# A four-layer graph network on one core: the first phase sums messages by a scan, ScalarE forms all product parts, gathers read kept index tables

## The reference: what is computed

```python
h = jnp.maximum(_layernorm(x, axis=-1), 0.0)
# layer 0: src, dst get a self loop for every node
deg = segment_sum(ones, dst);  dinv = rsqrt(deg)
xw = h @ W
agg = segment_sum(xw[src] * (dinv[src] * dinv[dst])[:, None], dst) + b
x = x + where(agg >= 0, agg, prelu_a * agg)
# layer 1: x = x + segment_sum(edge_weight * h[src], dst) @ W.T + b
# layer 2: attention over the incoming edges, batch norm over all nodes, relu
# layer 3: an edge network and a node network on the edges' end points, segment_sum, relu
```

## Time and profile before

| What | us |
|---|---|
| median of 3 runs | 2609.81 (2604.56 to 2611.62) |
| profiled execution, its own time | 2608.14 |
| span in it, first to last instruction | 2606.6 |

### The profile page before, as it was taken

One profiled execution on the slowest core, in us unless ns is written; L12 is line 12 of the kernel. 1 busy time (PEld: TensorE's weight loads), 2 busy tenths in 40 slices (PEclk: granted clock), 3 DMA queues, 4 the chain that ended last, 5 costly groups with the idle time before them and its releaser, 6 DMA issues. The chain is left out here.

```text
span 2606.6 us, 48448 instructions
## 1 busy us (share of the span) xinstructions
PE 1899.9 (73%) x9715; PEld 1275.5 (49%) x9715; DVE 2027.9 (78%) x8016; ACT 1725.7 (66%) x4230; POOL 1311.4 (50%) x1309
## 2 busy tenths in 40 slices
PE   2445668888855666578884899566663999999996
PEld 1134445555534555468883444233332555555553
DVE  6855579999968999688885888588885777777773
ACT  3655679999965777589991444699994444444441
POOL 6755656666637666277760000000002677777773
PEclk9878889999986888889996999799997999999998
DMA  7989986666645777556662443699996544445540
GB/s 134 220 147 183 153 203 193 198 195 195 194 130 159 222 223 224 176 165 198 201 181 72 128 129 86 185 305 308 305 308 215 128 100 107 106 113 114 115 106 21
DMA packets 376244, 446.18 MB, mean 171 GB/s; under 512 B 103667, under 2 KB 225338, under 8 KB 376082
## 3 DMA queue, kind: packets, MB, share of 16 engines
q1 hardware_dynamic: 309970, 368.09, 50.8%
q0 software_dynamic: 59840, 74.08, 12.3%
q10 hardware_dynamic: 6272, 2.06, 0.5%
HBM read 288.86 MB, written 185.03 MB: 182 GB/s over the span
## 5 line engine op out<-in xcount | busy, mean ns | idle before, releaser
L2380 POOL DMA_INDIRECT mlp_bx<-t_X,k_bslot x2 | 2.0, 1012 | 611.7 <-POOLq L2647 611.4
L526 POOL DMA_INDIRECT second_xs<-t_XX,second_irs x200 | 205.4, 1027 | 115.8 <-issue 49.3
L2398 POOL DMA_INDIRECT out_dram<-mlp_ou,mlp_iro x200 | 212.6, 1063 | 83.2 <-issue 71.3
L2391 POOL DMA_INDIRECT mlp_xs<-t_X,mlp_irs x200 | 213.8, 1069 | 80.7 <-issue 55.7
L526 POOL DMA_INDIRECT project_xs<-t_XX,project_irs x200 | 199.6, 998 | 62.9 <-issue 58.3
L526 POOL DMA_INDIRECT a_xd<-in_x_dram,a_ird x152 | 152.6, 1004 | 129.1 <-DVE first_xo L968 84.9
L2439 DVE TENSOR_TENSOR_SCAN mlp_ms<-mlp_fm,mlp_ms,mlp_mm 128x500 f32<-128x500 f32 x98 | 123.4, 1260 | 120.2 <-ACT mlp_mm L2515 112.9
L2515 ACT ACTIVATE mlp_mm<-mlp_ps_m,mlp_bn 128x500 f32<-128x500 f32 x100 | 67.7, 677 | 187.1 <-PE mlp_ps_m L2575 187.1
L2265 PE MATMUL x_ps_o<-x_ht,x_wd 128*128 128x512 f32 (+1 forms) x198 | 117.1, 675 | 97.2 <-DVE x_ht L2165 81.1
L2575 PE MATMUL mlp_ps_m<-mlp_e,mlp_wn 128*128 128x504 f32 x400 | 185.3, 586 | 0.0
L2562 PE MATMUL mlp_ps_e<-mlp_h,mlp_we 128*128 128x504 f32 x400 | 179.5, 592 | 2.9 <-DVE mlp_h L2448 1.5
(11 more groups left out here) (411 smaller groups left out, 6343.3 us busy)
## 6 DMA issues: line engine op xcount, KB each, us to landing
first_x<-in_x_dram SPq DMA_DIRECT2D x97, 256.0 KB, 4.3
t_XX<-first_x SPq DMA_DIRECT2D x97, 256.0 KB, 2.7
project_x<-t_XX SPq DMA_DIRECT2D x97, 256.0 KB, 3.3
x_x<-t_XX SPq DMA_DIRECT2D x97, 256.0 KB, 4.3
t_X<-x_x SPq DMA_DIRECT2D x97, 256.0 KB, 3.7
out_dram<-x_ou SPq DMA_DIRECT2D x97, 256.0 KB, 4.7
t_XR<-in_x_dram SPq DMA_DIRECT2D x23, 1000.0 KB, 13.4
t_G<-second_g SPq DMA_DIRECT2D x50, 267.8 KB
```

Source lines behind the costliest of these rows:

```text
L526: pool.indirect_dma_start(dst[:, q, lo:hi], None, table, bass.IndirectOffsetOnAxis(ap=idx[:, q:q + 1], axis=0)).then_inc(s_rows, 16)
L2391: pool.indirect_dma_start(Xs[u][:, q, :], None, T["X3"], bass.IndirectOffsetOnAxis(ap=irs[u][:, q:q + 1], axis=0)).then_inc(s_rows[u], 16)
L2398: pool.indirect_dma_start(out, bass.IndirectOffsetOnAxis(ap=iro[s][:, q:q + 1], axis=0), OU[s][:, q, :], None, bounds_check=N - 1, oob_is_ ...
```

## The change

Three things are changed.

1. **First phase, edge sum.** The selection product, the carry product and the one-row copies are gone. ACT forms M and Hd of all four tiles in a row at the head of its body; PE turns M and adds turned Hd by identity products (`turned`); one scan per round on DVE (`summed`) multiplies by a mask and adds, over 504 slots, and carries its last column into the next round. The scan writes AT itself, so ACT's copy `at` is gone. Hd's scale `dinv2` is multiplied by `lastc` in `prep`, so that the own row is added only at the last slot. SP loads the mask `fr` every round, broadcast to 128 partitions; that load waits for the scan two groups back. The edge product gets a PSUM bank of its own (psQ, in the place of the carry's).
2. **Prelu parts.** The parts of half 0 are now formed by ACT too (`parts(g1, 0)`, ahead of `rows(t, u, 0)`), and DVE combines them as it does those of half 1.
3. **Gather indices.** The copies into `irs`, `ird`, `iro` are gone in four phases (but for the first groups' early gathers). POOL reads the kept tables, for which its loops are unrolled.

```diff
-        dve.tensor_tensor(kp.dinv2[:, :], kp.dinvc[:, :], kp.dinvc[:, :], ALU.mult)
+        done(dve.tensor_tensor(kp.dinv2[:, :], kp.dinvc[:, :], kp.dinvc[:, :], ALU.mult))
+        dve.tensor_tensor(kp.dinv2[:, :], kp.dinv2[:, :], kp.lastc[:, :], ALU.mult)
...
+            if there(t, NGE):
+                r = u % 2
+                if not before(t, 2):
+                    gate(kp, sp, e_at, t - 1)
+                sp.dma_start(fr[r][:, :].rearrange("p (k j) -> p k j", k=GT),
+                             T["f5"][bass.ds(t * GT, GT), :].partition_broadcast(128)).then_inc(e_fr[r], 16)
...
-            gate(kp, pool, e_idx, t + 1)
+            src, dst = kp.srci[:, t * GT:(t + 1) * GT], kp.dsti[:, t * GT:(t + 1) * GT]
...
-        steps(pool, NGE, 10, 0, body)
+        straight(NGE, 0, body)
...
+        def summed(g, r):
+            if there(g, NGE):
+                dve.wait_ge(e_fr[r], landed(g, r, 2))
+                dve.wait_ge(e_a, g + 1)
+                if not before(g, 2):
+                    dve.wait_ge(e_y, g - 1)
+                if not before(g, 1):
+                    dve.wait_ge(e_at, g)
+                init = 0.0 if before(g, 1) else AT[1 - r][:, W4 - 1:W4]
+                dve.tensor_tensor_scan(AT[r][:, :], fr[r][:, :], psA[:, 0:W4], init, ALU.mult, ALU.add).then_inc(e_at, 1)
...
-                if there(g, XG) and h == 1:
+                if there(g, XG):
                     dve.wait_ge(s_q[h], t + 1)
                     dve.scalar_tensor_tensor(feat(Rp[h], g), feat(Qp[h], g), kp.oma[:, 0:1], feat(Rp[h], g),
                                              ALU.mult, ALU.add).then_inc(s_p[h], 1)
-                if there(g, XG) and h == 0:
-                    dve.wait_ge(s_z, g + 1)
-                    if not before(g, 2):
-                        dve.wait_ge(s_b, g - 1)
-                    dve.tensor_scalar(feat(Qp[h], g), featps(psZ, g), kp.nb0[:, 0:1], kp.noma[:, 0:1], ALU.min, ALU.mult).then_inc(s_q[h], 1)
-                    dve.wait_ge(s_q[h], t + 1)
-                    dve.scalar_tensor_tensor(feat(Rp[h], g), feat(Qp[h], g), kp.low0[:, 0:1], featps(psZ, g),
-                                             ALU.add, ALU.add).then_inc(s_p[h], 1)
...
-            edge_rows(g1, s1, 0)
-            carry(g1, r1, 0)
+            for q in range(GT):
+                edge_rows(g1, s1, q)
...
-            edge_rows(g1, s1, 1)
-            carry(g1, r1, 1)
             ht(g1, 1)
-            edge_rows(g1, s1, 2)
-            carry(g1, r1, 2)
...
-            edge_rows(g1, s1, 3)
-            carry(g1, r1, 3)
+            parts(g1, 0)
             rows(t, u, 0)
             parts(g1, 1)
-            if there(g1, NGE):
-                act.wait_ge(e_a, g1 + 1)
-                if not before(g1, 1):
-                    act.wait_ge(e_y, g1)
-                act.activation(AT[:, :, :], psA[:, 0:W4].rearrange("p (q e) -> p q e", q=GT), ACT.Copy).then_inc(e_at, 1)
...
+            for q in range(GT):
+                pe.wait_ge(e_hd, t * GT + q + 1)
+                ag = psA[:, q * RW:(q + 1) * RW]
+                pe.matmul(ag, M[r][:, q, :], kp.ident[0:RW, 0:RW], start=True, stop=False)
+                ins = pe.matmul(ag, Hd[r][:, q, :], kp.ident[0:RW, 0:RW], start=False, stop=True)
+            ins.then_inc(e_a, 1)
...
-                gather_rows(pool, Xs[u], T["XX"][0:ROWS, :], irs[u], s_rows[u])
-
-        steps(pool, NGE, 1, 0, body)
+                gather_rows(pool, Xs[u], T["XX"][0:ROWS, :], kp.idx[:, t * GT:(t + 1) * GT], s_rows[u])
+
+        straight(NGE, 0, body)
...
-            indices(t + 3, (u + 3) % 4)
```

125 lines of the change are left out of this document (30 added, 95 removed).

## The result

| | Before | Changed |
|---|---|---|
| median | 2610.32 us (2604.56 to 2611.62, 4 runs) | 2654.62 us (2647.05 to 2657.92, 4 runs) |
| ratio, 95% interval | | 1.0168 (1.0148 to 1.0188) |
| profiled execution, its span | 2608.14, 2606.6 | 2647.05, 2645.5 |

A forecast was written before the change was run, and what follows sets the result against it. ACT was taken to bound the late first phase. Order +23.5, mask load +11, drain +1, `prep` +0.3, second -3 and starts -2 gave +31 us on 2608.14; median forecast 2640 us, 8-in-10 range 2617 to 2662.

The forecast's parts named there:

- What bounds the kernel: ACT sets the late first phase with DVE 94% full behind it; transfers the early rounds, DVE second, PE mlp.
- ACT's work, 10.74, and DVE's, 10.39: First-phase work per round after the change: ACT from 10.67 to 10.74 us, DVE from 10.22 to 10.39.
- The order: Late first phase: ACT waits for `mv` or PE's half 0 product; 0.67 us per round, 35 rounds, +23.5 us.
- The mask load: Early first phase, where transfers set the pace: 0.93 us per added load, 12 rounds, +11 us (bounds 4 and 19).
- Second: Second phase: one index copy less per round on DVE, 0.06 us x 50 = -3 us.
- Project: Project phase, ACT's: index copies hidden behind the full engine, so 0 us.
- 1 (waits absorbed): Late first phase: ACT's round is its work, 10.74 us; 2.5 us instead of 23.5, total 2619; chance 0.12.
- 2 (mlp follows POOL): Mlp follows POOL, not PE: some 48 rounds each lose 0.6 us, -29 us, total 2611; chance 0.06.
- 3 (the clock falls in the first phase): PE drops to 1.2 GHz in late first-phase rounds: +9 us (2649) for a quarter, +35 (2675) for all; chance 0.16.
- small terms: Drain of last two rounds +1 us, `prep` +0.3, second phase -3, starts of second and mlp -1 each.

The follow-up runs named there:

- z9: Kernel before with the second part alone: ACT forms both prelu parts of half 0, DVE combines them; 2680.0 us, ratio 1.0163.
- z10: Changed kernel, old first-phase order, but fourth tile's rows ahead of `sd` and its turning ahead of half 1's turning back and product; 2630.6 us, ratio 1.0075.
- y7: Changed kernel with DVE's combination of Re and Qe moved behind the variances `mv`; 2683.5 us, ratio 1.0174 to the kernel before.
- y5: Changed kernel with `ht` of half 0 at the head of ACT's body and its product first on PE; 2696.4 us, ratio 1.0223 to the kernel before.
- y2: Changed kernel with its first phase back in the old order of work on ACT and PE, new operations kept; 2678.6 us, ratio 1.0165 to the kernel before.
- z8: Changed kernel with the old first-phase order, but the fourth tile's rows ahead of `sd` on ACT; 2679.7 us, ratio 1.0162 to the kernel before.
- y4: Changed kernel with the scan's mask loaded for the first two groups only, 48 loads left out, sums wrong; 2664.3 us, ratio 1.0114 to the kernel before.
- z1: Kernel before with the third part alone: indices straight from the kept tables, POOL unrolled; 2633.3 us, ratio 0.9990.
- x1: Kernel before with kept index tables and unrolled POOL alone, run in the slow first group; 3080.15 us, ratio 1.0016 to 3067.24 us.

## Why the prediction was right, point by point

- **What bounds the kernel.** Right: ACT in the late first phase. z9 shows it directly: work added to ACT alone comes out in full (11.90 for 11.82).
- **ACT's work, 10.74, and DVE's, 10.39.** Right for ACT: where no wait is left (z10) the round is 10.72 in the median and was 10.67 before, +0.05 for the +0.07 of the steps. The figures of the Trainium skill's page "ScalarE: Activation LUTs", section "What ACT_TABLE_LOAD costs", would have made it shrink by 0.09 a round instead; the trace does not agree with that. DVE's scan took 0.04 more than forecast. The operations that the change takes from DVE for half 0 were two (L939, L941), as the prediction counts, and not the three of the description above it.
- **The order.** Right in mechanism, place and size: +24.9 us for +23.5 (the waits come out in full, and the forecast's 0.67 a round measured 0.71), `sd` waiting 0.55 us for `mv`, DVE 0.99 us for Qe, the product of half 0 ending 0.07 ahead of `rp`. y7 and y5 took away one path each and found the other. What the forecast did not see is that a third loop, of DVE and PE alone, lies ready behind them at 11.31 once the order of ACT is put back (y2, z8). It had no part in the changed kernel, where all four tiles are turned early, and so did no harm to the number.
- **The mask load.** Mechanism right, the term too small: +14.7 for +11 in the same pair of profiles, inside its bounds of 4 and 19. The step that was too small is the price per load: 0.93 us, from the queue's mean over the whole span. At that stretch's own mean rate it was 1.48, and y4 against y2, y5 and y7 measured 1.4 to 1.7 us. The rate of the stretch in which a transfer is added is the one to take. In the pair itself 14.7 us over 11 rounds are 1.34 a load at most; up to 3 of them may be the new order (206.9 in y4 against 204.4 in z1), though z10 does not bear that out.
- **Second.** -2.6 for -3 in this pair; over all profiles about -2, not clear of their spread. **Project.** Forecast 0, measured +4.9, of which 3.6 come from the kept tables (profiles with and without). The step "the copies there are hidden behind full engines, 0" missed that the unrolled POOL stream could cost something. The trace says where: the steady round is 5.28 us on ACT before and after, while the first seven rounds (by ACT's `project_he`) take 39.3 and 40.3 us without the kept tables and 41.1 to 42.1 with them, about half of the difference. Why stays open: the gathers of a group are issued 5.2 to 5.3 us apart in both, close to ACT's pace there, and no run separates the causes.
- **The rivals.** 1 (waits absorbed): wrong, ACT's row has a gap in every round. 2 (mlp follows POOL): wrong; the gathers of 1.61 us are gone (the longest is 1.02 now) and POOL is busy 175.96 of 240 us for 183.94, yet the phase takes 525.5 us for 526.6. 3 (the clock falls in the first phase): wrong for the changed kernel, granted 1.00 from 390 to 770 us, with PE busy 75% of it and not the two thirds of the forecast; but in z10, y7 and z9 the clock did fall, below.
- **The remaining difference.** The sum gave +31 us; the profiled executions differ by 38.9, the medians by 44.3. The mask's 4 us, project's 5 and the late rounds' 1.4 make up the first, less some 2 us of small terms that ran the other way (x3 and mlp). The rest is that the changed kernel's profiled execution was the shortest of its four.
- **A version better than both** was not found. z1, the third part alone, is at 0.9990 with an interval that takes in no change. The steps say why the first two parts have little to give: per round, ACT and DVE together work 20.89 us before and 21.13 after, so even dealt out evenly 10.57 is the least after, where 10.45 was before; the scan takes work from PE, which had time to spare, and puts it on the two engines that had none.

## What to carry to other kernels

Before moving work, add up the two fullest engines together: a change that relieves a third one and loads these has little or nothing to win, however its pieces are dealt out. Then follow each engine's body in order past every hand-over and look for loops that close from one round to the next; a result that moves to another consumer (here the turned sum, from a late copy on ScalarE to the middle of VectorE's body) turns a harmless place in its producer's queue into part of such a loop. And price an added transfer by the rate of the stretch in which it is added.

## What the runs showed of the hardware that was not expected

**The same kernel, three times.** The kernel before took 2609, 2635 and 3067 us beside different groups. The record names the chip by a number: 3 for the first group, 15 for the y runs, 9 for z1, z8 and z9, and 15 again for z10. So the same number stands beside 2635 and 2609, and the chip alone does not tell the difference. In the 3067 us group, x1 shows which phases are longer than in the profile of the kernel before: late first rounds 13.59 us for 10.68, second 332.2 for 285.0, project 355.1 for 244.9, mlp 635.1 for 526.6; attend (194.5 for 195.4) and x3 (327.8 for 329.9) are not. The stretch ahead of the first round's `first_xo` is longer too (234.6 us for 175.3). The long phases are those with indirect gathers in every round; x3 has none and moves the most bytes, 302 GB/s in x1 and 305 in the kernel before, so the rate of plain transfers had not fallen there. The timeline of x1 shows a stop of all engines at once:

```profile
508.37 0.69 DVE L943 TENSOR_TENSOR first_x<-first_x,first_ps_b 128x512 f32<-128x512 f32 x1 [2.71 <-remote]
508.51 0.27 ACT L979 ACTIVATE first_m<-first_ps_carry 1x128 f32<-1x128 f32 x1 [2.35 <-remote]
...
508.88 0.46 PE L1105 MATMUL first_ps_carry<-first_m,k_S 126*126 126x128 f32 x2 [2.52 <-ACT first_m L979]
```

The profile names no instruction as what ended these waits, only "remote". What it is, no run shows. In z1, of a group with 2634 us, the 25 us more lie ahead of the late rounds: the first `first_xo` starts 10 us later (185.1 for 175.3), the early stretch takes 204 us for 189, and the late rounds keep their 10.70.

**TensorE's clock in the same stretch, in six orders of work.** In the changed kernel the granted clock was 1.00 throughout the late first phase, with PE busy 284 of 380 us. In z10, whose rounds are shorter (PE busy 231 of 300), it was 0.95: again and again it fell for a moment to half, the 1.2 GHz level. Such a moment and what follows it:

```profile
540.50:543.90 3.40, 3.40 (x13) 2.80 (x14) 3.40 (x18) 3.40 (x9) 2.60 (x3) 0.50 0.84 287
543.90:551.00 7.10, 5.28 (x30) 3.40 (x28) 6.54 (x21) 7.10 (x19) 5.00 (x5) 1.00 0.64 178
```

That fall cost nothing: the round in which it lies, 540.97 to 551.68, took 10.71 us. Of the 35 late rounds 29 take 10.73 us or less, many of them with a mean clock of 0.86. Five take 11.20 to 11.29, one in every six. In these the fall catches the product of half 0, which takes 1.99 us for 1.13; PE's later work is pushed back, and ACT waits for the product on psY:

```profile
564.30 1.99 PE L1073 MATMUL first_ps_z<-first_ht,k_w 128*128 128x512 f32 x2 [0.40 <-ACT first_ht L988]
...
570.21 0.69 ACT L997 ACTIVATE first_rp<-first_ps_y,k_b 128x512 f32<-128x512 f32 x1 [0.28 <-PE first_ps_y L1073]
```

Together the five run 2.7 us over, most of the 3.5 by which z10's 35 rounds missed 10.72 each. From 450 to 750 us z8 had 1.00, y2 0.96, y7 0.91 and z9 0.88. The Trainium skill, "TensorE: Matmul & The Clock Gate", section "A second HAM failure mode: psum-queue depth-cycling", names frequent short idle times between groups of matmuls as enough to make the clock go up and down. These runs show a clock that does so on a PE that pauses in every round, but not that the pauses are the cause: y2 and z8, which differ only in where ACT forms one tile's rows and have the same mean round of 11.39, had 0.96 and 1.00, and y4, with the changed kernel's own order on every engine, had 0.98 for its 1.00 there. What decides it no run shows. So rival 3 was a fair one to keep in the range.
